# The last pass on groups of 512 nodes: scaled sum written back into its PSUM bank, residual in four buffers

## The reference

```python
agg[n]  = dinv[n] * (g[n] + sum of g[src[e]] over the edges e with dst[e] == n)
h[n]    = relu(agg[n] + b3)
out[n]  = layernorm(x1[n] + h[n])        # over the 256 features, eps 1e-5
```

## Time and profile before

| | us |
|---|---|
| median of three timed runs | 4261.39 |
| the profiled execution's own time | 4236.74 |
| its span | 4235.0 |
| the last pass: first gather starts | 3557.36 |
| first matmul of the pass | 3567.39 |
| last gather issued, in the trace | 4215.07 |

### The profile page before, as it was taken

One profiled execution on the slowest core, in us unless ns is written; L12 is line 12 of the kernel. 1 busy time (PEld: TensorE's weight loads), 2 busy tenths in 40 slices (PEclk: granted clock), 3 DMA queues, 4 the chain that ended last, 5 costly groups with the idle time before them and its releaser, 6 DMA issues. The chain is left out here.

```text
span 4235.0 us, 107970 instructions
## 1 busy us (share of the span) xinstructions
PE 3771.7 (89%) x27934; PEld 3481.4 (82%) x27934; DVE 3713.5 (88%) x10654; ACT 2649.3 (63%) x6276; POOL 2170.3 (51%) x1972
## 2 busy tenths in 40 slices
PE   6639999999999889999688889869889988999999
PEld 1139999999999768888688888868888887888887
DVE  8838898889889799999788888868888887999999
ACT  0016666666666578888677878757878885444444
POOL 0035444444444000000477777757777775777776
PEclk9869999999999989999899999989999999999999
DMA  0055555555555299999677767747767776999999
GB/s 24 1 98 166 162 159 158 158 158 159 160 159 159 70 324 375 374 374 376 217 211 214 214 211 218 213 151 213 217 208 215 219 216 197 315 311 309 312 311 287
DMA packets 871189, 909.87 MB, mean 215 GB/s; under 512 B 154170, under 2 KB 770580, under 8 KB 871060
## 3 DMA queue, kind: packets, MB, share of 16 engines
q1 hardware_dynamic: 744400, 702.74, 50.8%
q0 software_dynamic: 94080, 205.13, 17.9%
q10 hardware_dynamic: 32580, 0.52, 0.5%
HBM read 651.69 MB, written 308.28 MB: 227 GB/s over the span
## 5 line engine op out<-in xcount | busy, mean ns | idle before, releaser
L462 POOL DMA_INDIRECT rows<-ga_scratch,node_i x980 | 1081.4, 1103 | 997.5 <-POOLq L598 699.6
L462 POOL DMA_INDIRECT rows<-x_in,node_i x490 | 518.5, 1058 | 671.6 <-DVE raw L915 476.8
L462 POOL DMA_INDIRECT rows<-gb_scratch,node_i x490 | 567.1, 1157 | 182.3 <-issue 171.9
L490 PE MATMUL gcn_agg_ps<-gcn_rows_hi,gcn_select 128*128 128x256 f32 x2156 | 576.5, 302 | 33.9 <-DVE gcn_rows_lo L1260 33.9
L490 PE MATMUL gcn_agg_ps<-gcn_rows_lo,gcn_select 128*128 128x256 f32 x2156 | 542.8, 286 | 0.0
L1380 PE MATMUL fin_agg_ps<-rows,fin_select 128*128 128x256 f32 x2156 | 530.8, 380 | 0.0
L1279 ACT CAST gcn_rows_hi<-rows 128x768 fp32r<-128x768 f32 (+1 forms) x392 | 286.2, 731 | 331.9 <-DMA rows<-ga_scratch,node_i 162.3
L1380 PEld LDWEIGHTS fin_agg_ps<-rows,fin_select 128*128 128x128 f32 x2156 | 410.8, 191 | 56.2
L490 PEld LDWEIGHTS gcn_agg_ps<-gcn_rows_hi,gcn_select 128*128 128x128 f32 x2156 | 419.4, 195 | 34.8 <-DVE gcn_rows_lo L1260 34.8
L517 PE MATMUL gcn_g_ps<-g_hi,gcn_ht_hi 128*128 128x256 f32 x1568 | 441.7, 282 | 0.7 <-ACT gcn_g L1298 0.7
L862 ACT ACTIVATE h1t_hi<-h1t_ps,b_sb 128x256 fp32r<-128x256 f32 x392 | 164.8, 471 | 439.0 <-issue 346.2
(11 more groups left out here) (158 smaller groups left out, 12314.2 us busy)
## 6 DMA issues: line engine op xcount, KB each, us to landing
own<-x_in SPq DMA_DIRECT2D x196, 256.0 KB, 3.0
h_scratch<-h2t SPq DMA_DIRECT2D x196, 256.0 KB, 2.2
h2t_in<-h_scratch SPq DMA_DIRECT2D x196, 256.0 KB, 3.9
x_sb<-x_in SPq DMA_DIRECT2D x196, 256.0 KB, 4.9
x_scratch<-x SPq DMA_DIRECT2D x196, 256.0 KB, 5.0
ga_scratch<-g_out SPq DMA_DIRECT2D x196, 256.0 KB, 5.1
gcn_own<-ga_scratch SPq DMA_DIRECT2D x196, 256.0 KB, 2.9
gb_scratch<-gcn_g SPq DMA_DIRECT2D x196, 256.0 KB
```

The source lines that it names most:

```text
L462: pool.indirect_dma_start(out=c["rows"][:, slot, b], out_offset=None, in_=source[:, :], in_offset=bass.IndirectOffsetOnAxis(ap=c["node"][: ...
L490: last = nc.tensor.matmul(out[:, j], select[:, b, j * P:(j + 1) * P], rows[:, pair.odd + b], start=n == 0, stop=n == len(terms) - 1)
```

## The change

The last pass works on quads where it worked on pairs. `Quad`, `quad_pipeline`, `quad_rows`, `load_quad` and `select_columns` are new; two groups of four quads are unrolled at the start, and groups 2 to 23 run in the hardware loop. Each buffer ring holds four quads (it held four pairs), the PSUM sum two quads in four banks (two pairs in two banks). The own, x1 and output DMAs move 512 KB each. DVE writes `h` back over the sum in PSUM instead of into an SBUF tile, and one residual instruction reads 1024 columns of it; PE may reuse the banks only after that residual, and its identity matmuls come ahead of the waits for gathered rows and selects. The selects of a quad are five compares of 256, 384, 384, 256 and 128 columns. The statistics and the aggregates follow one another after the selects. The other passes are unchanged (`gather_quads` gets the count as an argument).

```diff
+SPAN = [(0, 2), (0, 3), (1, 4), (2, 4), (3, 4)]
+def select_columns(nc, c, quad, select):
+    for b, (first, end) in enumerate(SPAN):
+        last = nc.vector.tensor_scalar(select[:, b, 0:(end - first) * P], c["iota32"][:, first * P:end * P],
+                                       c["place"][:, bass.ds(quad.q, 1), b], None, ALU.is_equal)
+    return last
...
-        own = m.sb("fin_own", [P, RING, 2, D])
-        x1 = m.sb("fin_x1", [P, RING, 2, D])
-        select = m.sb("fin_select", [P, RING, FIRST + 1, PAIR])
-        h = m.sb("fin_h", [P, 2, 2, D])
-        res = m.sb("fin_res", [P, RING, 2, D])
+        own = m.sb("fin_own", [P, QUAD_RING, 4, D])
+        x1 = m.sb("fin_x1", [P, QUAD_RING, 4, D])
+        select = m.sb("fin_select", [P, 2, BLOCKS, 3 * P])
+        res = m.sb("fin_res", [P, QUAD_RING, 4, D])
...
-        agg_ps = m.ps("fin_agg_ps", [P, 2, 2, D])
+        agg_ps = m.ps("fin_agg_ps", [P, 2, 4, D])
...
# SP
+                    if quad := at(0):
+                        s = quad.slot
+                        load_quad(sp, fast, own[:, s], source, dram["base"], quad, loaded[s], agg_done)
+                        if quad.has(QUAD_RING):
+                            sp.wait_ge(res_added, quad.before(QUAD_RING))
+                        sp.dma_start(x1[:, s], quad_rows(dram["x1"], quad.q)).then_inc(loaded[s], 16)
+                    if quad := at(5):
+                        sp.wait_ge(y_ready, quad.done())
+                        sp.dma_start(quad_rows(dram["out"], quad.q), y[:, quad.slot]).then_inc(stored[quad.slot], 16)
...
# PE
+                    if quad := at(1):
+                        b, s = quad.b, quad.slot
+                        pe.wait_ge(loaded[s], quad.landed(2))
+                        if quad.has(2):
+                            pe.wait_ge(res_added, quad.before(2))
+                        for j in range(4):
+                            nc.tensor.matmul(agg_ps[:, b, j], c["ident"][:], own[:, s, j], start=j % 2 == 0,
+                                             stop=False, skip_group_check=True)
+                        pe.wait_ge(gathered[s], quad.landed(BLOCKS))
+                        pe.wait_ge(select_done, quad.done())
+                        for j in range(4):
+                            blocks = range(max(j - 1, 0), j + 2)
...
+                        last.then_inc(agg_done, 1)
...
# DVE
+                    chosen, summed, scaled = at(0), at(2), at(3)
+                    if quad := summed:
+                        b = quad.b
+                        dve.wait_ge(agg_done, quad.done())
+                        for j in range(4):
                             last = nc.vector.scalar_tensor_tensor(
-                                out=h[:, b, j], in0=agg_ps[:, b, j], scalar=c["dinv"][:, bass.ds(pair.q * 2 + j, 1)],
+                                out=agg_ps[:, b, j], in0=agg_ps[:, b, j], scalar=c["dinv"][:, quad.tile(j)],
                                 in1=bias[:], op0=ALU.mult, op1=ALU.add)
                         last.then_inc(h_ready, 1)
...
# reciprocal of the quad at lag 3
-                        nc.vector.scalar_tensor_tensor(out=res[:, s], in0=h[:, b], scalar=0.0, in1=x1[:, s],
+                        nc.vector.scalar_tensor_tensor(out=res[:, s], in0=agg_ps[:, b], scalar=0.0, in1=x1[:, s],
                                                        op0=ALU.max, op1=ALU.add).then_inc(res_added, 1)
...
# shift of the quad at lag 3
+                    if quad := chosen:
+                        if quad.has(2):
+                            dve.wait_ge(agg_done, quad.before(2))
+                        select_columns(nc, c, quad, select[:, quad.b]).then_inc(select_done, 1)
+                    if quad := summed:
+                        b = quad.b
+                        dve.wait_ge(res_added, quad.done())
+                        for j in range(4):
+                            last = nc.vector.bn_stats(stats[:, b, j], res[:, quad.slot, j])
+                        last.then_inc(stats_done, 1)
+                        dve.wait_ge(stats_done, quad.done())
+                        if quad.has(2):
+                            dve.wait_ge(shift_ready, quad.before(2))
+                        nc.vector.memset(c["spare"][:, 1:2], 0.0)
+                        for j in range(4):
+                            last = nc.vector.bn_aggr(mv[:, b, j], stats[:, b, j])
+                        last.then_inc(mv_done, 1)
...
# ACT: square root of the quad at lag 2, four scalings of the quad at lag 4
```

More of the change, by code:

```diff
@@ L47 @@
 LN_EPS = 1e-5
+QUAD_PEEL = 2
+QUAD_MAX_LAG = 6
 ALU = mybir.AluOpType
@@ L450, in _, with __init__, done, before @@
                 nc.vector.tensor_scalar(c["place"][:], base[:], -1.0, None, ALU.add).then_inc(chain, 1)
-def gather_quads(nc, pool, c, source, gathered, rows_free):
+class Quad:
+    def __init__(self, group, place):
+        self.group, self.place = group, place
+        self.q = group * QUAD_RING + place
+        self.slot, self.turn, self.b = place, group, place % 2
+    def done(self, per=1):
+        return (self.q + 1) * per
+    def before(self, back):
+        return self.q + 1 - back
+    def has(self, back):
+        return not isinstance(self.q, int) or self.q >= back
+    def landed(self, dmas):
+        return (self.turn + 1) * (16 * dmas)
+    def tile(self, j):
+        return bass.ds(self.q * 4 + j, 1)
+def quad_pipeline(eng, step):
+    def group(number):
+        for k in range(QUAD_RING):
+            def quad_at(lag, k=k):
+                quad = Quad(number + (k - lag) // QUAD_RING, (k - lag) % QUAD_RING)
+                if isinstance(quad.q, int) and not 0 <= quad.q < NQ:
+                    return None
+                return quad
+            step(quad_at)
+    for number in range(QUAD_PEEL):
+        group(number)
+    with eng.Fori(QUAD_PEEL, NQ // QUAD_RING) as number:
+        group(number)
+    for number in range(NQ // QUAD_RING, -(-(NQ + QUAD_MAX_LAG) // QUAD_RING)):
+        group(number)
+def quad_rows(dram, q):
+    return dram[bass.ds(q * QUAD, QUAD), :].rearrange("(j p) d -> p j d", p=P)
+def load_quad(sp, fast, out, source, base, quad, landed, slot_free):
+    for ran, rows in ((1, source), (0, base)):
+        with sp.If(fast == ran):
+            if quad.has(QUAD_RING):
+                sp.wait_ge(slot_free, quad.before(QUAD_RING))
+            sp.dma_start(out, quad_rows(rows, quad.q)).then_inc(landed, 16)
+def gather_quads(nc, pool, c, source, gathered, rows_free, per):
     bound = pool.to_reg(NPAD - 1)
@@ L1345, in step @@
                 def step(at):
[L1346 to L1359, removed]
+                    if quad := at(0):
+                        s = quad.slot
+                        load_quad(sp, fast, own[:, s], source, dram["base"], quad, loaded[s], agg_done)
+                        if quad.has(QUAD_RING):
+                            sp.wait_ge(res_added, quad.before(QUAD_RING))
[3 more added lines that the diff above has]
+                        sp.dma_start(quad_rows(dram["out"], quad.q), y[:, quad.slot]).then_inc(stored[quad.slot], 16)
+                quad_pipeline(sp, step)
+                for s in range(QUAD_RING):
+                    sp.wait_ge(stored[s], 16 * len(range(s, NQ, QUAD_RING)))
             @block.gpsimd
             def _(pool):
-                gather_quads(nc, pool, c, source, gathered, agg_done)
+                gather_quads(nc, pool, c, source, gathered, agg_done, 1)
             @block.tensor
@@ L1367, in step @@
                 def step(at):
[L1368 to L1378, removed]
+                    if quad := at(1):
[10 more added lines that the diff above has]
+                            blocks = range(max(j - 1, 0), j + 2)
                             for k in blocks:
-                                last = nc.tensor.matmul(agg_ps[:, b, j], select[:, s, k, j * P:(j + 1) * P],
-                                                        c["rows"][:, pair.quad_slot, pair.odd + k],
-                                                        start=False, stop=k == blocks[-1])
+                                column = (j - SPAN[k][0]) * P
+                                last = nc.tensor.matmul(agg_ps[:, b, j], select[:, b, k, column:column + P],
+                                                        c["rows"][:, s, k], start=False, stop=k == blocks[-1],
+                                                        skip_group_check=True)
                         last.then_inc(agg_done, 1)
-                pipeline(pe, step)
+                quad_pipeline(pe, step)
             @block.vector
@@ L1404, in step @@
[L1404 to L1410 removed]
+                    if quad := scaled:
+                        b = quad.b
+                        dve.wait_ge(sd_ready, quad.done())
+                        nc.vector.reciprocal(rs[:, b], sd[:, b]).then_inc(rs_ready, 1)
```

97 lines of the change are left out of this document (38 added, 59 removed).

## The result

Five runs of the changed kernel have a median of 4237.84 us (4234.67 to 4241.66), five of the kernel before 4261.39 us (4258.61 to 4263.67). The ratio is 0.9945 with a 95% interval of 0.9931 to 0.9960, so the change saves 23.5 us. The forecast was 4251.8 us in a range of 4240 to 4265: right in sign, 14.0 us too slow, and outside its range by 2.2 us. The two intervals don't overlap.

The account below looks back on a forecast made before the run. The prediction took DVE to bound the last pass, by itself and through POOL. Its terms, -18.9 for freed gathers, +7.8 for selects and +1.5 for the tail, gave -9.6: 4261.4 to 4251.8 us, range 4240 to 4265.

Parts of the forecast that it names:

- The bound of the kernel before, and what lengthened its gathers: Last pass: DVE bounds, by itself and through POOL, whose gathers the residual's two SBUF inputs lengthen by what is left less 0.13.
- Removed, up to 18.9: Last pass's gathers: the residual, with one SBUF input, no longer holds POOL, saving up to 18.9 us.
- Selects, +7.8: Last pass: about one gather start per quad falls into the select run at random phase, 0.08 a quad, costing 7.8 us.
- rival 1: Last pass: the selects miss the gathers and POOL runs free, -17.4 us, 4244.0 us; chance 0.14.
- DVE's work per quad, 5.95 and about 6.1 in the loop: DVE in the last pass: summed instructions take 5.95 us a quad against 6.55, about 6.1 inside the hardware loop.
- Tail, 20.4: From the last gather's end to the span's end: 20.4 us in place of 18.9, +1.5.
- Sum, -9.6: Whole change: -18.9 for freed gathers, +7.8 for selects, +1.5 at the end, together -9.6 us.
- The carry from profile to median: Whole run: the profile's difference is added unchanged to the median, 24.65 us above the profiled run; good to some 3 us.
- 2: Last pass: another bound, PE or DMA, just under the old pace; quads settle at 6.65 to 6.72, about 4259 us; chance 0.21.
- 3: Last pass: DVE's select runs wait for whole gathers, 7.1 a quad, +39 us, 4300 us; chance 0.02.
- 4: Last pass: the residual still holds POOL, 0.39 a quad, +28 us, 4290 us; chance 0.03.
- 5: Last pass: the select run locks onto a gather each quad, 0.29 at full, +11.0 us, 4272 us; chance 0.10.

Follow-up runs that it names:

- p_psum: The kernel before, still on pairs, with h written back into PSUM (four bank slots) and the residual reading it there: 4249.26 us, ratio 0.9980.
- q_sbuf: The changed kernel with h in an SBUF tile, so the residual again has two SBUF inputs: 4270.91 us, ratio 1.0033.
- q_both: The changed kernel with four gathers per quad in place of five in the last pass and no identity matmuls: one run of 4196.95 us, 6.27 a quad.
- q_4g: The changed kernel with four gathers per quad in place of five in the last pass: one run of 4220.38 us, 6.479 a quad.
- after_same: The changed kernel measured once more, with an empty edit: 4236.47 us against 4247.71 for the kernel before, ratio 0.9973.
- q_noident: The changed kernel without the four identity matmuls of each quad, own rows loaded but not added: one run of 4230.25 us, 6.549 a quad.

## Why the prediction was off, step by step

*The bound of the kernel before, and what lengthened its gathers:* right. p_psum freed the gathers and DVE kept its pace. q_sbuf and the changed kernel differ in where one operand lies, and by 26.5 us of last pass. The arithmetic of a hold (what is left, less 0.13) gave 1.04 for q_sbuf's long gather, as measured.

*Removed, up to 18.9:* measured by the groups. Busy time of 490 gathers fell from 509.8 (490 x 1.040) to 493.8, with 490 x 1.001 = 490.5 as the least: 19.3 lost before, 3.3 after.

*Selects, +7.8:* over-sized, 3.3. The run of selects has the length worked out (1.38 from start to start, 4210.49 to 4211.87) and holds gathers as foreseen, 1.20 in place of 1.00. One start a quad falls into it, also as foreseen (99 in the pass). What failed is the random phase: 76 of the 99 began where 0.20 or less of their select was left, which holds them for 0.08 at most, and 34 of these with 0.13 or less, which holds them not at all. Why the phase settles there is not shown. 3.3 lies between the forecast's 7.8 and rival 1's 0. The pass became 15.8 us shorter; the sum had 11.1.

*DVE's work per quad, 5.95 and about 6.1 in the loop:* the first is right, the second 0.17 too low. In q_both, where DVE doesn't wait for PE after its first `h`, the first quads, ahead of the loop, lie 5.98 to 6.14 apart, and in the loop the pace is 6.27. The changed kernel agrees: 6.547 less 0.24 of waiting is 6.31. So the slack against POOL is 0.24 to 0.3 and not 0.4, which was still enough. The write-back, allowed 0 to 0.4, costs no time: four h take 1.58 from start to start (4207.58 to 4209.16), worked out 1.52, but they take 1.58 in q_sbuf too, which writes them to SBUF. The residual took 1.14 to the next start in place of 1.07, statistics and aggregates 1.82 in place of 1.70.

*POOL's pace, 6.55 to 6.65:* 6.56. PE's floor of 6.48 is q_4g's pace.

*Tail, 20.4:* 22.9 in the trace, 22.4 in after_same; +4.0 against +1.5. Two of its terms failed. First, 4.4 from POOL's end to PE, with the identity matmuls hidden: the row matmuls started at 4215.58, 5.65 after 4209.93. PE, 0.07 from POOL's pace, had no pause to hide them in; it went straight from them into the rows. Second, "four y, 2.1": ScalarE had eight scalings to do, 4.02, since in the order of its steps the y of quad 96 stands behind the square root of quad 97. The trace of before had it too: the last row counts four scalings, where a pair has two, so its 2.07 is for the last two pairs, and two quads make eight.

*Sum, -9.6:* -11.9 in the traces (677.6 to 665.7), and -11.2 by the medians of after_same. The mechanism is right, and its sum is within 2.3 us, in part by luck: the stretch of the gathers came out 4.7 us better than the sum had it and the tail 2.5 us worse.

*The carry from profile to median:* this is the step that failed. The text added a difference from one execution to a median 24.65 us above it, and held the measured time to about 0.2%. The changed kernel's profiled run was only 3.17 under its median, and 24.65 - 3.17 = 21.5 is, with the 2.1 between the two profiled runs, the 23.5 measured. Before-medians were 4261.4, 4257.5, 4247.7 and 4254.7 us in four measurements (the last three on different chips), a spread of 13.7 us for one file. The range allowed 3 us for this; it needed some 10. Two executions of before reach the last pass 15.7 us apart. Why the first measurement shows 12 us more than the second is open: the last pass of the two traces agrees within 1.0 us, so it does not seem to be there. Whether the larger SBUF tile or the longer program shifts the phase of the unchanged passes was not tried.

*Rivals.* 2 is refuted (6.547, not 6.65). 3 is refuted: DVE's selects didn't wait for gathers, since its pace less waiting is 6.31, not 7.1. The hold goes one way only in these traces. In before 71 gathers that began under a residual took over 1.05, and each lasted longer by what was left of it less 0.12 to 0.13; all 153 residuals that began inside a gather took their usual 0.69, among them the one 0.58 inside a gather of 1.00 (4205.92, 4206.50). With one of the residual's inputs in PSUM the hold was gone (90 gathers under L1484, none over 1.01). Two SBUF inputs are not all of it: a select has `iota` in SBUF as its one wide input, and under the selects of the changed kernel 31 of 99 gathers took over 1.05, up to 1.21, while under `bn_stats`, which reads `res` in SBUF, none of 95 took over 1.02. What sets these two apart is not shown. 4 is what q_sbuf does: its holds cost 31.3 us (worked out 38), and its last pass is 13.6 us longer than that of before (worked out +28, since 7.8 was set for the selects, under which gathers lose next to nothing there, 0.3). 5 is refuted in its price: the holds are 3.3 / 98 = 0.03 a quad, where it decides from 0.18. A phase that returns, which it argued, is there, but at the end of a select and not at its beginning.

## What to carry to other kernels

Where GpSimd issues gathers, look through the DVE instructions that run beside them for two SBUF inputs, and let the engine ahead write its result back into PSUM: here that edit took 7% and 8% off the two graph passes. Take the hold away only together with room on the engine that comes next (p_psum gained 0.2%, the same edit with shorter DVE work more), and read off each floor by taking the other engines' work away. At the end of a pipeline list every instruction behind the last result in the order of the engine's steps, those of earlier rounds too. And before a difference of some 10 us is forecast for a median, find out how far the executions and the medians of one file lie apart: here one execution 24.65 us under the median was the sign that 3 us would not cover it.

## What the runs showed of the hardware

- The residual's hold of POOL has a gap at its front. Timeline of the kernel before, DVE's residuals and POOL:

```profile
4203.29 0.74 DVE L1410 SCALAR_TENSOR_TENSOR fin_res<-fin_h,fin_x 128x512 f32<-128x512 f32 x1
...
4203.31 1.00 POOL L462 DMA_INDIRECT rows<-ga_scratch,node_i  x1 [0.30 <-issue]
...
4205.92 1.00 POOL L462 DMA_INDIRECT rows<-ga_scratch,node_i  x1 [0.31 <-issue]
```

A gather that started 0.02 after the residual kept 1.00, and the residual took 0.74 instead of 0.69. All 13 gathers of before that started within 0.06 of a residual (0.015 to 0.022 after it) were like this. In q_sbuf four that started up to 0.04 after kept 1.00, and one that started 0.05 after was held for 1.04.
- Writing h over its own PSUM input costs 9 ns on 128x256: 486 against the 477 of q_sbuf, whose order of instructions is the same (469 against 459 in pairs, p_psum and before). From start to start it costs nothing. A 128x1024 residual takes 1225 ns with its first input in PSUM and 1228 in SBUF. The 128x512 cast is the exception: 676 ns from PSUM against 421 from SBUF. Group of q_sbuf:

```profile
L1471 DVE SCALAR_TENSOR_TENSOR fin_h<-fin_agg_ps,dinv,gb_sb 128x256 f32<-128x256 f32 x392 | 162.6, 477 | 67.1 <-PE fin_agg_ps L1455 65.2 <-issue 0.5
```

- One file's executions on one chip lay between 4238.61 and 4278.06 us, and the two graph passes' stretches varied by themselves: a pass of 490 gathers took from 716.1 to 731.5 us in the traces of before.
- With work taken away from PE, the clock granted to it dropped at times. In four of the 25 stretches of 4 us between 3800 and 3900 of q_noident it was 0.56 to 0.59, and 1.00 in the others. Three windows of q_noident:

```profile
3836.00:3840.00 4.00, 2.03 (x10) 1.48 (x9) 3.84 (x12) 0.93 (x2) 3.08 (x4) 1.00 1.05 369
3840.00:3844.00 4.00, 4.00 (x12) 3.17 (x12) 3.85 (x15) 2.26 (x5) 3.08 (x4) 0.57 0.95 301
3844.00:3848.00 4.00, 2.99 (x15) 2.31 (x14) 3.96 (x18) 0.75 (x3) 3.08 (x4) 1.00 0.95 296
```

After 4 us in which PE was busy 2.03, the clock granted was 0.57, and 12 matmul records filled the next 4 us, where some 19 do at 1.00 (465 in 100 us in the changed kernel); in the 4 us after that it was 1.00 again. After 3876 to 3880, with PE busy 2.21, it stayed at 1.00, and in q_both, with the same matmuls left out, it was 1.00 over 3800 to 3900. What sets it is not shown. The pace was the same, 6.549 a quad against 6.547, since PE wasn't the bound.
